# b2 by a broadcast load, zero products ahead of the sums for q, T3's sum on GpSimd, T4 over T2

## The chip, the cores and the metric

One core of a Trainium2 chip. The time is device microseconds of one execution of the whole kernel; lower is better.

## The reference

```python
q_emb = relu(q @ W3 + b3)              # q: 64 x 512, W3: 512 x 1024
v_sum = sum(v, axis=1, keepdims=True)  # v = x: 64 x 128 x 1024
y = (128 * v + v_sum) * q_emb[:, None, :]
out = x + relu(y @ W2 + b2)            # W2: 1024 x 1024, b2: 1024, all float32
```

## The kernel before

**What it computes with.** x is scaled in place, per feature (partition) and batch row: y = scale * x + bias, with scale = 128 * q_emb and bias = v_sum * q_emb. A unit is two batch rows (t = 0, 1), a pair is two units (c = 0, 1): 16 pairs. The two row blocks t and the two halves of the features h make y a 2 x 2 block matrix, and W2 is cut in the same way into b11, b12, b21, b22. Each operand of TensorE is split in two numbers, hi = the value rounded to fp32r (ScalarE) and lo = value - hi (VectorE), and each block product is hi*hi + hi*lo + lo*hi over four slices k: 12 matmuls of 128x128 by 128x512. Pair 0 takes the 16 plain block products (`PLAIN_PRODUCTS`). Pairs 1 to 15 take the 7-product scheme of Strassen and Winograd, 14 products a pair in the order `ORDER` (m = 1, 5, 6, 2, 7, 3, 4, each for c = 0 and 1; "step i" below). It needs four sums of weights: T1 = b12 - b11, T2 = b22 - T1, T3 = b22 - b12, T4 = b21 - T2 up to sign. Each is made once, in fp32, in a staging buffer, and then split into hi and lo. All weights stay in the SBUF for the rest of the run.

**Staging.** Three pairs of halves of 128x1024: `w_halves` (b11, T1, T2), `v_halves` (b12, T3) and `u_halves` (b21, b22, b21 again, T4). `u_halves` are also the buffers `u2_sb` and `m5_sb` of the pairs.

**Order.** Nothing is scheduled by a planner: the order of each engine is written out by hand, with semaphores. The start is: W3 by four slices, the first quarter of x, b11 in four pieces (SyncE's queue); on TensorE four products of zeros (`mark`), the row b2 spread over 128 partitions by a product with a row of ones, then the sums for q (`q_sum(k)`, four of eight before the first product, the others behind it), zero products between and behind them (`WARM_UP`), and then the plain products. ScalarE copies b2 out of PSUM to `b_first` and `b_step`, makes q_emb (`q_relu`), rounds (`cast_w`, `cast_first`), scales (`scale_first`, `scale_usual`) and writes b2 into the banks that a product adds to (`seed_plain`, `seed_p`, `seed_r`). VectorE sums x over its rows (`sums_0`, `scalars_usual`), makes the lo parts (`low_w`, `low_first`, `low`), the sums of weights (`w_sum`) and the results (`plain_result`, `c11` and so on). GpSimd scales three quarters of x and makes b_step - b_first. Every engine works its own list in order; a late instruction holds up all that stands behind it in that list.

Behind `low_first(8)` VectorE's list is: low b22, sum T3, scalars of unit 3 (`scalars_usual(1, 1, 1)`), sum T2, low T3, then pair 1. Ahead of it stand low b12, sum T1, scalars of unit 2, four plain results and low T1. In pair 1, at step 4 both halves of T4 are summed, at step 6 their lo parts follow. Product i = 2 (m = 5, c = 0) needs `seed_r(1, 0)`, which ScalarE does ahead of cast 5 and behind the plain result that VectorE does at step 4; product i = 8 (m = 7, c = 0) needs `save_u2(1, 1, 0)`, which ScalarE does ahead of cast 11.

Of the kernel before, what the change touches and what calls it, by code (L numbers as in the profile page):

```python
# [5 lines left out]
def cond_residual(nc, x_t, x, small_t, b2, w3_t, w2_q, out):  # L6
# [38 lines left out]

    SPLIT = [("b11", 4), ("b21", 2), ("b12", 2), ("t1", 2), ("b22", 2), ("t3", 2), ("t2", 2), ("t4", 2)]
# [8 lines left out]
    with ctx:  # L55
# [3 lines left out]
        def sem(name):  # L59
# [15 lines left out]
        ones = sb("ones", [1, P])  # L75
# [13 lines left out]
        b2_row = w_extra[0:1].rearrange("p k m -> p (k m)")  # L89
# [4 lines left out]
                 "b21": u_halves, "b22": u_halves, "t4": u_halves}  # L94

        small_loaded, b2_loaded = sem("small_loaded"), sem("b2_loaded")
# [13 lines left out]
        table_set, warm_set, ones_set = sem("table_set"), sem("warm_set"), sem("ones_set")  # L110
        marked, b_sent, b_copied, b_seeded, b_step_ready = sem("marked"), sem("b_sent"), sem("b_copied"), sem("b_seeded"), sem("b_step_ready")
# [3 lines left out]
        t1_ready, t2_ready, t3_ready, t4_ready = sem("t1_ready"), sem("t2_ready"), sem("t3_ready"), sem("t4_ready")  # L115
        x0_scaled = [sem(f"x0_scaled{n}") for n in range(QUARTERS)]
# [61 lines left out]
        def _(sp):  # L178
# [7 lines left out]
            def load_half(name, kh, mh, h, loaded):  # L186
                half = slice(h * 2 * MH, (h + 1) * 2 * MH)
                sp.dma_start(STAGE[name][h], w2_q[kh, mh, :, half]).then_inc(loaded[h], 16)
# [10 lines left out]
            load_b11(0)  # L199
            load_b11(1)  # L200
# [7 lines left out]
            for h in range(2):  # L208
                load_half("b21", 1, 0, h, b21_loaded)
# [12 lines left out]
            for h in range(2):  # L222
                sp.wait_ge(w_lo_ready, split("b21", h))
                load_half("b22", 1, 1, h, b22_loaded)

            for h in range(2):
                sp.wait_ge(w_lo_ready, split("b22", h))
                sp.wait_ge(t3_ready, h + 1)
                sp.wait_ge(t2_ready, h + 1)
                load_half("t4", 1, 0, h, b21_again)  # L230
# [46 lines left out]
        def _(pe):  # L277
# [3 lines left out]
            def q_sum(k):  # L281
                pe.wait_ge(w3_loaded[k], 16)
                bank = Q_BANKS[k] if k < KH else 1
                for t in range(QT):
                    last = nc.tensor.matmul(acc[:, bank, k * B:(k + 1) * B], w3_stage[:, k, t], cond_sb[:, t],  # L285
                                            start=k < KH and t == 0, stop=False, skip_group_check=True)
                last.then_inc(q_summed, 1)

            def mark(bank, start=False):

                return nc.tensor.matmul(acc[:, bank], warm[:, :P], warm[:], start=start, stop=False, skip_group_check=True)  # L291

            pe.wait_ge(warm_set, 1)
            for bank in (3, 6, 2, 4):
                mark(bank, start=True)
            pe.wait_ge(ones_set, 1)
            pe.wait_ge(b2_loaded, 16)
            add(acc[:, 3], ones[:], b2_row[:, :MH])
            add(acc[:, 6], ones[:], b2_row[:, MH:]).then_inc(b_sent, 1)
            pe.wait_ge(small_loaded, 16)  # L300
            for k in range(KH):
                q_sum(k)
                if k < KH - 1:
                    mark(4)
            for _ in range(WARM_UP):
                mark(2)
            for n, bank in enumerate(Q_BANKS):
                pe.wait_ge(q_ready, n + 1)
                last = mark(bank)
            last.then_inc(marked, 1)  # L310

            for n, (o, name, bank) in enumerate(PLAIN_PRODUCTS):
                if n > 0:
                    pe.wait_ge(lo_ready, o + 1)
                if n == 0:
                    pe.wait_ge(b_copied, 1)
                if n in (1, 2, 3):
                    pe.wait_ge(b_seeded, n)
                if bank == 6:
                    pe.wait_ge(b_copied, 2)  # L320
                if bank == 7 or bank < 2:
                    pe.wait_ge(b_seeded, {7: 4, 0: 5, 1: 6}[bank])
# [52 lines left out]
        def _(act):  # L375
            def cast_first(n):
                q, c, place = MADE[n]
                act.wait_ge(x0_scaled[n % QUARTERS], 1)
                if n == QUARTERS:
                    act.wait_ge(x0_scaled[0], 2)  # L380
# [4 lines left out]
                if n == 0:  # L385
                    half = KH // 2
                    nc.scalar.copy(a_hi[:, place, :half], quarter(c, q)[:, :half]).then_inc(hi_started, 1)
                    act.wait_ge(x0_scaled[0], 2)
                    nc.scalar.copy(a_hi[:, place, half:], quarter(c, q)[:, half:]).then_inc(hi_ready, 1)
                else:  # L390
                    nc.scalar.copy(a_hi[:, place], quarter(c, q)).then_inc(hi_ready, 1)  # L391
# [63 lines left out]
            def save_m5(p, c):  # L455
                act.wait_ge(prod_done, done_by(p, 5, c))
                if isinstance(p, int) and p == 1:
                    act.wait_ge(w_lo_ready, split("t4", 1))
# [4 lines left out]
            def save_u2(p, parity, c):  # L463
                act.wait_ge(prod_done, done_by(p, 6, c))
                if not (isinstance(p, int) and p == 1):
# [13 lines left out]
            act.dma_start(b2_row, b2).then_inc(b2_loaded, 16)  # L479
# [3 lines left out]
            act.wait_ge(b_sent, 1)  # L483
            nc.scalar.copy(b_first[:], acc[:, 3]).then_inc(b_copied, 1)
            nc.scalar.copy(b_step[:], acc[:, 6]).then_inc(b_copied, 1)
# [7 lines left out]
            act.wait_ge(b_copied, 2)  # L493
# [4 lines left out]
            act.wait_ge(q_ready, KH)  # L498
            seed_plain(4, b_first)
            for k in range(KH, KT):  # L500
                q_relu(k)
            scale_first(2)
            cast_first(2)
# [7 lines left out]
            seed_plain(7, b_step)  # L511
            seed_plain(0, b_step)
# [7 lines left out]
            for h in range(2):  # L520
                cast_w("t1", h, t1_ready, h + 1)
            for n in range(3):
                scale_usual(1, 1, n)
            for c in range(2):
                seed_p(1, 1, c)
            cast_first(8)
            for h in range(2):
                cast_w("b22", h, b22_loaded[h], 16)
            for h in range(2):
# [4 lines left out]
            def pair(p, parity, following=True):  # L534
                first = isinstance(p, int) and p == 1
                for i in range(STEPS):
# [14 lines left out]
                    if first and i == 6:  # L551
# [17 lines left out]
        def _(pool):  # L569
# [7 lines left out]

            for n in (3, 4, 6):
                scale_first(n)

            pool.wait_ge(b_seeded, 6)
# [3 lines left out]
        def _(dve):  # L585
# [115 lines left out]
            nc.vector.memset(ones[:], 1.0).then_inc(ones_set, 1)  # L701
# [3 lines left out]
            for k in range(KH):  # L705
                last = nc.vector.tensor_scalar(x_sb[:, 0, 0, k], x_sb[:, 0, 0, k], scale[:, 0, 0, k:k + 1],
                                               bias[:, 0, 0, k:k + 1], ALU.mult, ALU.add)
                if k % 2 == 1:
                    last.then_inc(x0_scaled[0], 1)
# [5 lines left out]
            low_w("b11", 1)  # L715
            dve.wait_ge(hi_ready, 1)
            low_part(place, KH // 2, KH, quarter(c, q)).then_inc(lo_ready, 1)
            sums_0(1)
            low_w("b11", 2)
            scalars_0(1)  # L720
            low_w("b11", 3)
# [5 lines left out]
            sums_0(4)  # L727
            scalars_0(4)
            low_first(2)
# [13 lines left out]
            for h in range(2):  # L743
                low_w("b12", h)

# [3 lines left out]
            scalars_usual(1, 1, 0, x1_loaded[0], 16)  # L749
            plain_result(4, 0, 0, 0, c11_done)  # L750
            plain_result(5, 0, 1, 0, c21_done)
            for h in range(2):
                low_w("t1", h)
            plain_result(6, 1, 0, 0, c11_done)
            plain_result(7, 1, 1, 0, c21_done)
# [3 lines left out]

            for h in range(2):  # L760
# [11 lines left out]
            def pair(p, parity, loads=None):  # L772
# [3 lines left out]
                for i in range(STEPS):  # L776
# [27 lines left out]
                    if first and i == 6:  # L804
# [58 lines left out]
```

## Time and profile before

| | |
|---|---|
| median of 3 runs | 649.77 us (649.77 to 649.79) |
| profiled execution: time, span | 649.77 us, 648.0 us |
| TensorE busy | 636.9 us, 2795 matmuls |
| VectorE, ScalarE, GpSimd busy | 445.0, 420.9, 7.7 us |
| matmuls of block products | 2712 = 226 products x 12 |

A row of the timeline gives start and length in us, engine, line, operation, what it writes and reads, its shape, how often it stands in a row, and in brackets the idle time ahead of it with what ended it. Matmuls are pipelined: what a matmul costs in a stream is the distance from start to start, not its length.

### The profile page before, as it was taken

Reading aid. Unit: us, or ns where it says so; the run is one execution under the profiler, and the core shown is the slowest. Engines: PE = TensorE matmul, PEld = TensorE weight load, DVE = VectorE, ACT = ScalarE, POOL = GpSimd, SP = SyncE. Lnnn points to the kernel's source line nnn. Section 1 sums busy time; section 2 is a strip of 40 time slices with the busy share of each in tenths; the row PEclk is TensorE's granted clock in tenths of the full one; section 3 lists DMA queues with packets and bytes.
Section 4 is the critical chain, followed back from the end, with each engine's and each line's share of the span. In section 5 each row is a group of like instructions: output and inputs, shape, how many; then the busy total and the mean of one; then the engine's idle time right before and its main releaser. Section 6 shows DMA issues by size and latency. Waiting matters only on the chain.

```text
span 648.0 us, 9257 instructions
## 1 busy us (share of the span) xinstructions
PE 636.9 (98%) x2795; PEld 522.5 (81%) x2796; DVE 445.0 (69%) x675; ACT 420.9 (65%) x902; POOL 7.7 (1%) x17
## 2 busy tenths in 40 slices
PE   9898999999999999999999999999999999999997
PEld 6786778888888888888888888888888888888886
DVE  1788888777576767757677675767767576876633
ACT  2777778765939576593957759395674948668320
POOL 0220000000000000000000000000000000000000
PEclk9999999999999999999999999999999999999999
DMA  8741474637354353735335373433636443360603
GB/s 305 305 177 27 168 244 178 229 147 243 130 194 138 148 168 129 259 129 188 123 150 186 129 256 132 166 123 159 199 129 229 159 150 118 161 218 1 234 25 129
DMA packets 27232, 108.31 MB, mean 167 GB/s; under 512 B 3025, under 2 KB 3153, under 8 KB 23378
## 3 DMA queue, kind: packets, MB, share of 16 engines
q1 hardware_dynamic: 27072, 108.02, 46.5%
q10 hardware_dynamic: 146, 0.14, 0.1%
q8 instruction: 5, 0.08, 0.1%
q14 instruction: 9, 0.07, 0.0%
HBM read 74.59 MB, written 33.55 MB: 167 GB/s over the span
## 4 chain that ended last, share of the span: by engine, by line
PE 88%; ACT 6%; DVE 5%; issue 1%; ACTq 0%; DVEq 0%
PE acc L279 86%; ACT x_sb L409 3%; PE acc L285 2%; DVE vsum L587 1%; DVE w_lo L655 1%; ACT w_hi L428 1%; ACT a_hi L391 1%; DVE a_lo L650 1%; PE acc L291 0%; ACT a_hi L404 0%; DVE w_stage L659 0%; ACT acc L477 0%; DVE xn L663 0%; ACT q_emb L473 0%; DVE m_sb L659 0%
## 5 line engine op out<-in xcount | busy, mean ns | idle before, releaser
L279 PE MATMUL acc<-w_hi,a_hi 128*128 128x512 f32 x904 | 352.6, 390 | 6.4 <-DVE a_lo L639 3.6
L279 PE MATMUL acc<-w_lo,a_hi 128*128 128x512 f32 x904 | 351.7, 389 | 0.0
L279 PE MATMUL acc<-w_hi,a_lo 128*128 128x512 f32 x904 | 351.7, 389 | 0.0
L409 ACT ACTIVATE x_sb<-x_sb,bias,scale 128x128 f32<-128x128 f32 x496 | 204.8, 488 | 12.0 <-DVE bias L595 12.0
L279 PEld LDWEIGHTS acc<-w_hi,a_hi 128*128 128x128 f32 x904 | 169.7, 188 | 44.2 <-DVE a_lo L639 4.4
L279 PEld LDWEIGHTS acc<-w_hi,a_lo 128*128 128x128 f32 x904 | 169.7, 188 | 35.4
L279 PEld LDWEIGHTS acc<-w_lo,a_hi 128*128 128x128 f32 x904 | 169.7, 188 | 34.8
L650 DVE TENSOR_TENSOR a_lo<-x_sb,a_hi 128x512 fp32r<-128x512 f32 x150 | 103.5, 690 | 109.3 <-ACT a_hi L404 108.7
L404 ACT CAST a_hi<-x_sb 128x512 fp32r<-128x512 f32 x150 | 93.5, 623 | 40.1 <-PE acc L279 38.1
L404 ACT CAST a_hi<-s 128x512 fp32r<-128x512 f32 x60 | 37.5, 624 | 73.2 <-PE acc L279 69.1
L587 DVE TENSOR_REDUCE vsum<-x_sb 128x16 f32<-128x2048 f32 (+1 forms) x38 | 73.8, 1942 | 6.8 <-DMA x_sb<-x_t 6.8
L663 DVE SCALAR_TENSOR_TENSOR xn<-acc,xn 128x512 f32<-128x512 f32 x68 | 46.6, 689 | 35.4 <-PE acc L279 35.4
L453 ACT COPY acc<-acc 128x512 f32<-128x512 f32 x30 | 17.1, 571 | 50.1 <-PE acc L279 50.1
L650 DVE TENSOR_TENSOR a_lo<-s,a_hi 128x512 fp32r<-128x512 f32 x60 | 41.3, 688 | 0.1
L679 DVE TENSOR_TENSOR m_sb<-m_sb,acc 128x512 f32<-128x512 f32 x30 | 20.6, 688 | 23.2 <-PE acc L279 21.9
L689 DVE TENSOR_TENSOR u_sb<-u_sb,acc 128x512 f32<-128x512 f32 x30 | 20.6, 688 | 8.4 <-PE acc L279 8.4
L663 DVE SCALAR_TENSOR_TENSOR xn<-m_sb,xn 128x512 f32<-128x512 f32 x30 | 20.6, 686 | 0.2
L629 DVE TENSOR_TENSOR s<-s,x_sb 128x512 f32<-128x512 f32 x30 | 20.6, 686 | 0.1
L663 DVE SCALAR_TENSOR_TENSOR xn<-u_sb,xn 128x512 f32<-128x512 f32 x30 | 20.6, 686 | 0.1
L625 DVE TENSOR_TENSOR s<-x_sb 128x512 f32<-128x512 f32 x30 | 20.6, 686 | 0.0
L631 DVE TENSOR_TENSOR x_sb<-x_sb 128x512 f32<-128x512 f32 x30 | 20.5, 685 | 0.0
L635 DVE TENSOR_TENSOR x_sb<-x_sb,s 128x512 f32<-128x512 f32 x30 | 20.5, 685 | 0.0
(51 smaller groups left out, 195.9 us busy)
## 6 DMA issues: line engine op xcount, KB each, us to landing
xn<-x SPq DMA_DIRECT2D x64, 512.0 KB, 4.0
out<-xn SPq DMA_DIRECT2D x62, 512.0 KB, 4.2
x_sb<-x_t SPq DMA_DIRECT2D x30, 1024.0 KB, 5.0
x_sb<-w_t SPq DMA_DIRECT2D x8, 256.0 KB, 5.4
x_sb<-x_t SPq DMA_DIRECT2D x8, 256.0 KB, 7.8
u_sb<-w_q SPq DMA_DIRECT2D x3, 512.0 KB, 7.5
m_sb<-w_q SPq DMA_DIRECT2D x3, 512.0 KB, 7.6
w_stage<-w_q SPq DMA_DIRECT2D x4, 256.0 KB, 6.2
```

What stands on the lines that cost most here:

```text
L279: return nc.tensor.matmul(dst, lhs, rhs, start=False, stop=False, skip_group_check=True)
L404: nc.scalar.copy(a_hi[:, i % RING], operand(m, 2 * parity + c, c)).then_inc(hi_ready, 1)
L409: last = nc.scalar.activation(x_sb[:, slot, t, k], x_sb[:, slot, t, k], ACT.Identity, bias=bias[:, slot, t, k:k + 1], scale=scale[:, slot, ...
L587: nc.vector.tensor_reduce(vsum[:, slot, t0:t1, k0:k1], x_sb[:, slot, t0:t1, k0:k1], AX.X, ALU.add).then_inc(vsum_ready, 1)
L625: last = nc.vector.tensor_tensor(s, a21, a22, ALU.add)
L629: last = nc.vector.tensor_tensor(s, s, a11, ALU.subtract)
L631: last = nc.vector.tensor_tensor(a21, a11, a21, ALU.subtract)
L635: last = nc.vector.tensor_tensor(a12, a12, s, ALU.subtract)
L650: nc.vector.tensor_tensor(a_lo[:, i % RING], operand(m, 2 * parity + c, c), a_hi[:, i % RING].bitcast(fp32), ALU.subtract).then_inc(lo_rea ...
L663: nc.vector.scalar_tensor_tensor(o, bank, 0.0, o, ALU.max, ALU.add).then_inc(ready, 1)
L679: nc.vector.tensor_tensor(m5_sb[:, c], m5_sb[:, c], p_bank(parity, c), ALU.add).then_inc(c22_summed, 1)
L689: nc.vector.tensor_tensor(u2_sb[:, c], u2_sb[:, c], r_bank(c), ALU.add).then_inc(c12_summed, 1)
```

## The change

- b2 comes in by two broadcast loads on SyncE's queue (`load_b`), 128 partitions x 512 each: `b_first` behind the first piece of b11, `b_step` ahead of b12. The row of ones, its two products and ScalarE's two copies are gone, and so is the wait of SyncE's queue for them. The load of b3 and q (`small_t`) is now the first on ScalarE's queue.
- TensorE starts with eight zero products in a row (one for each bank) in place of four and the two of b2; one more follows each of the four sums for q, and then `WARM_UP` = 11, without waits for q_emb.
- The first quarter of x is scaled by VectorE (two slices) and GpSimd (two slices); its second lo part comes ahead of the lo part of b11's second piece. q_emb's second half is made after quarter 2 is scaled and rounded.
- Product (8, b12) comes after (2, b12). b22 is split ahead of T1; ScalarE rounds quarter 8 and b22 ahead of T1.
- T3's sum runs on GpSimd, ahead of b_step - b_first.
- T4 is made over T2 in `w_halves`, one half at step 5 and one at step 6; it is rounded at step 7 and its lo part is made at step 8. `save_m5` and `save_u2` of pair 1 wait for T4's sum.

```diff
-    WARM_UP = 5
+    WARM_UP = 11
@@ SyncE
             load_first(0)
             load_b11(0)
+            load_b(b_first, 0, b_first_loaded)
             load_b11(1)
...
-            sp.wait_ge(b_sent, 1)
+            load_b(b_step, 1, b_step_loaded)
             for h in range(2):
-                load_half("b12", 0, 1, h, b12_loaded)
+                load_half(v_halves, 0, 1, h, b12_loaded)
@@ TensorE
-            for bank in (3, 6, 2, 4):
-                mark(bank, start=True)
-            pe.wait_ge(ones_set, 1)
-            pe.wait_ge(b2_loaded, 16)
-            add(acc[:, 3], ones[:], b2_row[:, :MH])
-            add(acc[:, 6], ones[:], b2_row[:, MH:]).then_inc(b_sent, 1)
+            for n in range(8):
+                nc.tensor.matmul(acc[:, n], warm[:, :P], warm[:], start=True, stop=True)
             pe.wait_ge(small_loaded, 16)
             for k in range(KH):
                 q_sum(k)
-                if k < KH - 1:
-                    mark(4)
-            for _ in range(WARM_UP):
-                mark(2)
-            for n, bank in enumerate(Q_BANKS):
-                pe.wait_ge(q_ready, n + 1)
-                last = mark(bank)
-            last.then_inc(marked, 1)
+                keep_warm(1)
+            keep_warm(WARM_UP).then_inc(marked, 1)
@@ ScalarE
-            cast_first(0)
+            cast_first_half(0)
+            act.wait_ge(b_first_loaded, 16)
+            seed_plain(3, b_first)
+            cast_first_half(1)
...
+            for n in range(2):
+                scale_usual(1, 1, n)
+            cast_first(8)
+            for h in range(2):
+                cast_w("b22", h, b22_loaded[h], 16)
             for h in range(2):
                 cast_w("t1", h, t1_ready, h + 1)
-            for n in range(3):
-                scale_usual(1, 1, n)
+            scale_usual(1, 1, 2)
@@ GpSimd
+            pool.wait_ge(scalars_first, 1)
+            for k in range(KH // 2, KH):
+                last = nc.gpsimd.tensor_scalar(x_sb[:, 0, 0, k], x_sb[:, 0, 0, k], scale[:, 0, 0, k:k + 1],
+                                               bias[:, 0, 0, k:k + 1], ALU.mult, ALU.add)
+            last.then_inc(x0_scaled[0], 1)
...
+            for h in range(2):
+                pool.wait_ge(b22_loaded[h], 16)
+                pool.wait_ge(w_lo_ready, split("b12", h))
+                pool.wait_ge(t1_ready, h + 1)
+                nc.gpsimd.tensor_tensor(v_halves[h], u_halves[h], v_halves[h], ALU.subtract).then_inc(t3_ready, 1)
@@ VectorE
             for h in range(2):
                 low_w("b12", h)
+            scalars_usual(1, 1, 0, x1_loaded[0], 16)
...
                 w_sum(w_halves, v_halves, w_halves, h, t1_ready)
-            scalars_usual(1, 1, 0, x1_loaded[0], 16)
+            low_first(8)
+            for h in range(2):
+                low_w("b22", h)
             plain_result(4, 0, 0, 0, c11_done)
             plain_result(5, 0, 1, 0, c21_done)
-            for h in range(2):
-                low_w("t1", h)
             plain_result(6, 1, 0, 0, c11_done)
             plain_result(7, 1, 1, 0, c21_done)
-            low_first(8)
-            for h in range(2):
-                low_w("b22", h)
-
-            for h in range(2):
-                dve.wait_ge(w_lo_ready, split("b12", h))
-                dve.wait_ge(t1_ready, h + 1)
-                w_sum(v_halves, u_halves, v_halves, h, t3_ready)
+            for h in range(2):
+                low_w("t1", h)
             scalars_usual(1, 1, 1, x1_loaded[1], 16)
...
-                    if first and i == 4:
-
-                        dve.wait_ge(t2_ready, 2)
-                        for h in range(2):
-                            dve.wait_ge(b21_again[h], 16)
-                            w_sum(u_halves, u_halves, w_halves, h, t4_ready)
-                    if first and i == 6:
+                    if first and i in (5, 6):
+
+                        h = i - 5
+                        dve.wait_ge(w_lo_ready, split("t2", h))
+                        dve.wait_ge(b21_again[h], 16)
+                        w_sum(w_halves, u_halves, w_halves, h, t4_ready)
+                    if first and i == 8:
                         for h in range(2):
                             low_w("t4", h)
```

## Rows read from the trace of the kernel before

**Rows 1.** The page: busy time by engine, and the chain that ended last.
```profile
PE 636.9 (98%) x2795; PEld 522.5 (81%) x2796; DVE 445.0 (69%) x675; ACT 420.9 (65%) x902; POOL 7.7 (1%) x17
PE 88%; ACT 6%; DVE 5%; issue 1%; ACTq 0%; DVEq 0%
```

**Rows 2.** The chain in order of time, its last long piece (start us, us, what).
```profile
95.03 549.73 PE acc L279 x2424
```

**Rows 3.** Waits of TensorE from 0 to 100 us (us in total, times, longest).
```profile
PE acc L279 <- DVE a_lo L639: 3.6, 2, 2.5
PE acc L279 <- DVE a_lo L650: 1.3, 1, 1.3
PE acc L279 <- ACT acc L445: 1.1, 1, 1.1
```

**Rows 4.** Timeline of TensorE, 0 to 25 us.
```profile
1.20 1.89 PE L291 MATMUL acc<-warm 128*128 128x512 bf16 x4 [1.20 <-DVE warm L699]
3.02 3.78 PE L279 MATMUL acc<-w_extra,ones 1*128 1x512 f32 x4
12.96 1.81 PE L285 MATMUL acc<-small_sb,x_sb 128*128 128x64 f32 x8
14.56 2.77 PE L291 MATMUL acc<-warm 128*128 128x512 bf16 x6
17.55 0.66 PE L291 MATMUL acc<-warm 128*128 128x512 bf16 x2 [0.22 <-DVE a_lo L639]
18.28 0.40 PE L279 MATMUL acc<-w_lo,a_hi 128*128 128x512 f32 x1
21.43 3.68 PE L285 MATMUL acc<-small_sb,x_sb 128*128 128x64 f32 x32
```

**Rows 5.** Timeline of ScalarE and VectorE, 14 to 17 us.
```profile
14.81 0.38 ACT L473 ACTIVATE q_emb<-acc,small_sb 128x64 f32<-128x64 f32 x1 [1.65 <-PE acc L285]
15.49 1.12 DVE L706 TENSOR_SCALAR x_sb<-x_sb,scale,bias 128x128 f32<-128x128 f32 x4
16.51 0.69 DVE L655 TENSOR_TENSOR w_lo<-w_stage,w_hi 128x512 fp32r<-128x512 f32 x1
```

**Rows 6.** DMA issues, 5.0 and 7.8 us (KB each, us to landing).
```profile
w_stage<-w_q SPq DMA_DIRECT2D x1, 256.0 KB, 6.8
x_sb<-x_t SPq DMA_DIRECT2D x1, 256.0 KB, 7.4
```

**Rows 7.** Timeline of GpSimd and VectorE, where both work.
```profile
35.72 0.45 POOL L574 TENSOR_SCALAR x_sb<-x_sb,scale,bias 128x128 f32<-128x128 f32 x1
34.78 0.96 POOL L574 TENSOR_SCALAR x_sb<-x_sb,scale,bias 128x128 f32<-128x128 f32 x1
34.80 0.69 DVE L639 TENSOR_TENSOR a_lo<-x_sb,a_hi 128x512 fp32r<-128x512 f32 x1
37.11 1.29 DVE L639 TENSOR_TENSOR a_lo<-x_sb,a_hi 128x512 fp32r<-128x512 f32 x2 [1.62 <-ACT a_hi L391]
38.16 1.39 POOL L582 TENSOR_TENSOR b_step<-b_step,b_first 128x512 f32<-128x512 f32 x1 [1.99 <-ACT acc L477]
39.11 1.53 DVE L655 TENSOR_TENSOR w_lo<-s,w_hi 128x1024 fp32r<-128x1024 f32 x1 [0.70 <-ACT w_hi L428]
40.56 1.21 DVE L655 TENSOR_TENSOR w_lo<-w_extra,w_hi 128x1024 fp32r<-128x1024 f32 x1
```

**Rows 8.** Timeline of VectorE and ScalarE, 52 to 95 us.
```profile
52.80 0.69 DVE L639 TENSOR_TENSOR a_lo<-x_sb,a_hi 128x512 fp32r<-128x512 f32 x1 [1.68 <-ACT a_hi L391]
58.30 2.28 DVE L587 TENSOR_REDUCE vsum<-x_sb 128x16 f32<-128x2048 f32 x1
60.82 4.74 ACT L409 ACTIVATE x_sb<-x_sb,bias,scale 128x128 f32<-128x128 f32 x12 [1.35 <-DVE bias L595]
74.91 0.59 ACT L445 COPY acc<-b_step 128x512 f32<-128x512 f32 x1 [0.58 <-DVE xn L663]
94.35 0.58 ACT L467 COPY u_sb<-acc 128x512 f32<-128x512 f32 x1
```

More of the change, by code:

```diff
@@ L42, in cond_residual @@
                       (4, "b21", 3), (5, "b21", 2), (6, "b21", 4), (7, "b21", 5),
[1 row of a table removed]
[1 row of a table added]
                       (5, "b22", 6), (7, "b22", 7), (4, "b22", 0), (6, "b22", 1)]
-    SPLIT = [("b11", 4), ("b21", 2), ("b12", 2), ("t1", 2), ("b22", 2), ("t3", 2), ("t2", 2), ("t4", 2)]
+    SPLIT = [("b11", 4), ("b21", 2), ("b12", 2), ("b22", 2), ("t1", 2), ("t3", 2), ("t2", 2), ("t4", 2)]
     W_PLACE = {"b11": W_SLOT[1], "b21": W_SLOT[2], "b12": W_SLOT[4], "t1": W_SLOT[5], "b22": W_SLOT[3],
                "t3": W_SLOT[7], "t2": W_SLOT[6], "t4": W_SLOT[4]}
-    WARM_UP = 5
+    WARM_UP = 11
     Q_BANKS = (0, 1, 7, 5)
@@ L93, in cond_residual @@
         STAGE = {"b11": w_halves, "t1": w_halves, "t2": w_halves, "b12": v_halves, "t3": v_halves,
-                 "b21": u_halves, "b22": u_halves, "t4": u_halves}
-        small_loaded, b2_loaded = sem("small_loaded"), sem("b2_loaded")
+                 "b21": u_halves, "b22": u_halves, "t4": w_halves}
+        small_loaded = sem("small_loaded")
+        b_first_loaded, b_step_loaded = sem("b_first_loaded"), sem("b_step_loaded")
         w3_loaded = [sem(f"w3_loaded{s}") for s in range(KT)]
@@ L184, in load_w3, with load_half, load_b @@
                 sp.dma_start(w3_stage[:, k], w3_t[k]).then_inc(w3_loaded[k], 16)
-            def load_half(name, kh, mh, h, loaded):
+            def load_half(halves, kh, mh, h, loaded):
                 half = slice(h * 2 * MH, (h + 1) * 2 * MH)
-                sp.dma_start(STAGE[name][h], w2_q[kh, mh, :, half]).then_inc(loaded[h], 16)
+                sp.dma_start(halves[h], w2_q[kh, mh, :, half]).then_inc(loaded[h], 16)
+            def load_b(dst, h, loaded):
+                sp.dma_start(dst[:], b2[:, h * MH:(h + 1) * MH].broadcast_to([P, MH])).then_inc(loaded, 16)
             def load_xn(u, c, t):
@@ L223, in _ @@
                 sp.wait_ge(w_lo_ready, split("b21", h))
-                load_half("b22", 1, 1, h, b22_loaded)
+                load_half(u_halves, 1, 1, h, b22_loaded)
             for h in range(2):
@@ L284, in q_sum, with keep_warm @@
                 for t in range(QT):
-                    last = nc.tensor.matmul(acc[:, bank, k * B:(k + 1) * B], w3_stage[:, k, t], cond_sb[:, t],
-                                            start=k < KH and t == 0, stop=False, skip_group_check=True)
+                    last = add(acc[:, bank, k * B:(k + 1) * B], w3_stage[:, k, t], cond_sb[:, t])
                 last.then_inc(q_summed, 1)
-            def mark(bank, start=False):
-                return nc.tensor.matmul(acc[:, bank], warm[:, :P], warm[:], start=start, stop=False, skip_group_check=True)
+            def keep_warm(n):
+                for _ in range(n):
+                    last = add(acc[:, 2], warm[:, :P], warm[:])
+                return last
             pe.wait_ge(warm_set, 1)
-            for bank in (3, 6, 2, 4):
-                mark(bank, start=True)
-            pe.wait_ge(ones_set, 1)
-            pe.wait_ge(b2_loaded, 16)
-            add(acc[:, 3], ones[:], b2_row[:, :MH])
-            add(acc[:, 6], ones[:], b2_row[:, MH:]).then_inc(b_sent, 1)
+            for n in range(8):
+                nc.tensor.matmul(acc[:, n], warm[:, :P], warm[:], start=True, stop=True)
             pe.wait_ge(small_loaded, 16)
@@ L314, in _ @@
                     pe.wait_ge(lo_ready, o + 1)
[L315 to L322, printed above, removed]
+                if n < 4:
+                    pe.wait_ge(b_seeded, n + 1)
+                if bank >= 6 or bank < 2:
+                    pe.wait_ge(b_seeded, {6: 5, 7: 6, 0: 7, 1: 8}[bank])
                 place, pieces = MADE[o][2], dict(SPLIT)[name]
@@ L375, in _, with cast_first_half @@
         def _(act):
+            def cast_first_half(h):
+                q, c, place = MADE[0]
+                half = slice(h * KH // 2, (h + 1) * KH // 2)
+                act.wait_ge((x0_started, x0_scaled[0])[h], 1)
+                nc.scalar.copy(a_hi[:, place, half], quarter(c, q)[:, half]).then_inc((hi_started, hi_ready)[h], 1)
             def cast_first(n):
@@ L384, in cast_first @@
                     act.wait_ge(prod_done, (min(old) if n == 7 else max(old)) + 1)
[L385 to L391, printed above, removed]
+                nc.scalar.copy(a_hi[:, place], quarter(c, q)).then_inc(hi_ready, 1)
             def cast(p, parity, i):
@@ L464, in save_u2 @@
                 act.wait_ge(prod_done, done_by(p, 6, c))
-                if not (isinstance(p, int) and p == 1):
+                if isinstance(p, int) and p == 1:
+                    act.wait_ge(t4_ready, 2)
+                else:
                     act.wait_ge(c12_done, 2 * p + c - 1)
@@ L497, in _ @@
             cast_first(1)
-            act.wait_ge(q_ready, KH)
             seed_plain(4, b_first)
+            scale_first(2)
+            cast_first(2)
             for k in range(KH, KT):
                 q_relu(k)
-            scale_first(2)
-            cast_first(2)
+            act.wait_ge(q_ready, KH)
             seed_plain(5, b_first)
@@ L510, in _ @@
             cast_first(5)
-            seed_plain(7, b_step)
-            seed_plain(0, b_step)
+            act.wait_ge(b_step_loaded, 16)
+            for bank in (6, 7, 0):
+                seed_plain(bank, b_step)
             scale_first(7)
@@ L528, in _ @@
                 cast_w("b22", h, b22_loaded[h], 16)
+            for h in range(2):
+                cast_w("t1", h, t1_ready, h + 1)
+            scale_usual(1, 1, 2)
+            for c in range(2):
+                seed_p(1, 1, c)
             for h in range(2):
@@ L550, in pair @@
                             cast_w("t2", h, t2_ready, h + 1)
-                    if first and i == 6:
+                    if first and i == 7:
                         for h in range(2):
@@ L704, in _ @@
             dve.wait_ge(scalars_first, 1)
-            for k in range(KH):
+            for k in range(KH // 2):
                 last = nc.vector.tensor_scalar(x_sb[:, 0, 0, k], x_sb[:, 0, 0, k], scale[:, 0, 0, k:k + 1],
                                                bias[:, 0, 0, k:k + 1], ALU.mult, ALU.add)
-                if k % 2 == 1:
-                    last.then_inc(x0_scaled[0], 1)
+            last.then_inc(x0_started, 1)
             q, c, place = MADE[0]
@@ L714, in _ @@
             low_part(place, 0, KH // 2, quarter(c, q)).then_inc(lo_started, 1)
-            low_w("b11", 1)
             dve.wait_ge(hi_ready, 1)
             low_part(place, KH // 2, KH, quarter(c, q)).then_inc(lo_ready, 1)
+            low_w("b11", 1)
+            low_w("b11", 2)
+            low_w("b11", 3)
             sums_0(1)
-            low_w("b11", 2)
             scalars_0(1)
-            low_w("b11", 3)
             sums_0(2)
@@ L758, in _ @@
                 low_w("b22", h)
+            plain_result(4, 0, 0, 0, c11_done)
+            plain_result(5, 0, 1, 0, c21_done)
+            plain_result(6, 1, 0, 0, c11_done)
+            plain_result(7, 1, 1, 0, c21_done)
             for h in range(2):
-                dve.wait_ge(w_lo_ready, split("b12", h))
-                dve.wait_ge(t1_ready, h + 1)
-                w_sum(v_halves, u_halves, v_halves, h, t3_ready)
+                low_w("t1", h)
             scalars_usual(1, 1, 1, x1_loaded[1], 16)
```

33 lines of the change are left out of this document (8 added, 25 removed), and 2 rows, old and new, of the table PLAIN_PRODUCTS.

## The prediction
> **What bounds the kernel now.** The page comes first: TensorE is busy for 98% of the span and holds 88% of the chain that ended last [rows 1]. The chain in order of time then says where the rest lies: from 95.03 us to the end TensorE works without a gap, 2424 matmuls in 549.73 us, 0.2268 us each [rows 2]. That stretch is the same code in both kernels; it can only move. So the question is how early pair 1's product 8 starts, which before is at 95.03 us. All 2712 matmuls at that pace are 615.1 us; they begin at about 18.0 [rows 4] and end at 644.8, so 11.7 us are lost ahead of 95. The waits of TensorE name 6.0 of them: 3.6 for lo parts of pair 0 (one of 2.5), 1.3 and 1.1 in pair 1 [rows 3]. Some 3.5 are the second four sums for q, which stay [rows 4]. The timelines give the chains behind these waits. The profiled execution took 649.77 us, which is also the median of the runs; 1.77 us lie outside its span of 648.0.
>
> **The sums for q.** Before, four zero products (1.20 to 3.0) and b2's two products (3.02 to 6.8) stand ahead of them. A sum takes 1.6 us there and a zero product 0.43 us, the last sum ends at 14.8 and q_emb is there at 15.2 [rows 4, 5]. The zero product's 0.43 us for 512 columns is the 1.2 GHz level; the real products are 0.23 us apart from 18.28 on and the four later sums take 3.68 / 4 = 0.92 us each, the 2.4 GHz level [rows 4]. So before, all sums ahead of the first product ran at the lower level, and it rose some 3.1 us after TensorE had begun nine zero products in a row at 14.56. After, eight stand in a row at 1.20, 3.4 us of the same work with no thin product behind it. I take the rise at about 4.3, the eight done at 4.5, and then four sums with three zero products between them: 4 x 0.92 + 3 x 0.22 = 4.35, to 8.85. q_emb is ready at 9.25, 5.9 us earlier. The loads allow it: the load issued at 5.0 lands at 11.8 and the one at 7.7 lands at 15.1, five places later, so one of 256 KB takes 0.66 us [rows 6]; W3's fourth slice is six places ahead of the former and lands by 7.8, when its sum is due at 7.9. The Trainium skill (TensorE: Matmul & The Clock Gate, "What's actually happening") has the low clock as the default that activity releases; no row shows whether eight zero products are enough, and that is the first rival.
>
> **Product 0.** VectorE scales two slices (2 x 0.28) and makes b11's first lo part, to 10.75, and x's first, to 11.1. Twelve zero products at 0.215 end at 11.45, where product 0 starts. GpSimd's two slices cost 0.45 each when alone, but it sat out VectorE's subtraction at 34.8 (0.96 in place of 0.45) although it had begun first [rows 7]. So I let it begin at 11.1 when VectorE pauses: 12.0, second rounding to 12.45, then b11's second piece: rounded 12.95, lo part 13.66. Lower bound 0.9 us earlier, if GpSimd is not held. Pieces 3 and 4 land 0.66 later than before for the broadcast, at 12.4, and follow at 14.25 and 14.9. Product 0 ends at 15.7, the four sums for q at 19.4 (before 25.1). Both b loads are 256 KB: 0.66 us each in the queue, under others' slack; that both halves of b2 are no longer copied takes 1.1 us from ScalarE, which idled there.
>
> **Pair 0.** Products follow at 12 x 0.2268 = 2.72 us: product 2 at 22.15 where before it was at 29.0. I followed each list with durations of its rows. The smallest margins: lo part 4 is ready some 0.2 us ahead of product 4, lo part 8 three us ahead of product 11. The 2.5 us wait is gone, since quarter 8 is rounded before T1 and used one product later; the other wait (1.1) goes because VectorE has the lo part by 21.3. Product 8 ends at 41.2, product 15 at 60.2.
>
> **T3 on GpSimd.** It frees VectorE of 2 x 1.14 us. Its own price no row shows. Nearest is the 512-wide subtraction: it began at 38.16, VectorE was busy to 38.40, it ended at 39.55: 1.15 us alone; twice that is 2.3 for 1024, upper bound 2 x 1.39 = 2.8. I take 2.25. And it holds VectorE: the lo part at 39.11 took 1.53 where its twin took 1.21 [rows 7]. Rounding 8 must wait for product 8: 41.2 to 41.85. T3's first half runs 39.7 to 41.95 in VectorE's pause, lo part 8 ends at 42.65, and as b22's rounding is not out until 42.85, GpSimd gets in with the second half, to 44.9: 2.0 us lost on VectorE. Bounds: nothing, if VectorE comes first, and 2.8. Behind it b_step - b_first (1.15) is queued, and it alone is behind it; I take that it finds VectorE's plain results (one input from PSUM) and costs nothing.
>
> The Trainium skill (SBUF — State Buffer, "Who interferes with whom") says that a VectorE instruction with two SBUF inputs and a GpSimd instruction that reads SBUF exclude each other whole, and that the order of issue decides who waits. By that rule b_step - b_first, issued at 44.9 while lo b22's first half starts, goes ahead of the second half. The 34.8 us pair speaks against it. This is a rival below.
>
> **VectorE and ScalarE to pair 1.** From 44.9 on VectorE works through: lo b22 2.3, four plain results 2.4, lo T1 2.3, scalars of unit 3 2.4 [the sum alone is 2.28, rows 8], to 54.2. ScalarE then has twelve scalings, 4.7 [rows 8], rounding 0 (59.5), four scalings, rounding 1 (61.6), T2's roundings 1.9, four scalings 1.6, rounding 2 (65.65). VectorE: lo 2 (66.3), sum (67.1), lo 3 (67.7), plain result 12 (68.3); seed_r (69.0). Products 0 and 1 of the pair start on time, product 2 is due at 60.2 + 5.44 = 65.7 and waits until 69.0: a new stall of 3.3 us. Before, that seed ended at 75.5 [rows 8], so product 2 is 6.6 us earlier. T4 no longer stands behind it, so seed_r(1) is in time and the wait of 1.1 is gone. From 68.3 on, VectorE has 7.6 us of steps 4 to 7 with T4 and then 2.4 of scalars; ScalarE behind them three times four scalings, three roundings and three saves, 7.5: save_u2 is done at 85.8 (before 94.93). Product 8 is due at 69.0 + 6 x 2.72 = 85.3 and starts at 85.85.
>
> **The sum.** 95.03 - 85.85 = 9.2 us. 649.77 - 9.2 = 640.6 us, ratio 0.986. The early clock moves the whole of pair 0 by some 6 us; in pair 1 VectorE's list, not TensorE's, then sets the time, so what GpSimd blocks is paid one for one.
>
> **Rivals.**
> - *The clock stays at 1.2 GHz through the sums* (0.16). For it: before, four zero products in a row did not raise it, and neither did 8 us of sums with single ones between. Against it: nine did. Then the eight end at 4.6, the four sums at 12.3, twelve zero products at 16.4 to 17.4, product 0 at 20.1, the sums at 23.8: 4.4 us behind the forecast, 645.0 at most, 644.0 at least.
> - *GpSimd does not hold VectorE* (0.10). T3's second half falls beside the plain results. VectorE gains 2.0: 638.6; with the early start of product 0 also 637.7, with all bounds 637.
> - *GpSimd's b_step also goes first* (0.10): 1.15 more, 641.8.
> - *The broadcast load is slow* (slower; 0.02). Its 128 partitions read one row of 2 KB. It stands ahead of b11's second piece, which lands at about 10.0 and is wanted at 12.45. Each us over 2.4 is paid in full; at 0.66 + 2.4 + 9.2 = 12.3 us for the load it is no gain, and beyond it slower. Against it: rows of 256 KB at 0.66, and the 2 KB a partition is the size of the others.
> - *Nothing moves* (0.03): lists that meet in pair 1 so late that the early start is given back. For it: VectorE bounds pair 1. Against it: its list is 2.3 us shorter and begins 6 us earlier.
>
> **How the numbers follow.** The forecast has 0.59, the rivals 0.16, 0.10, 0.10, 0.02, 0.03. Likeliest 640.6. The range goes from 636.9 (no blocking, all bounds) to 645.2 (the clock stays low), and leaves out some 0.07. 0.2% is 1.3 us, about what a measurement can tell from no change. Faster by more: 0.59 + 0.16 + 0.10 + 0.10 = 0.95; same 0.03; slower 0.02.
>
> **What would show it.** Sums for q 0.92 us each from 4.5 on and q_emb at 9.3: the clock; 1.6 each: the first rival. Product 0's second slice at 13.7 if GpSimd is held, 12.8 if not. No waits of TensorE from 20 to 60. GpSimd's T3: two of 2.25 us, and a lo part of b22 that is 3.2 in place of 1.2. A wait of 3.3 us ahead of pair 1's product 2, behind ScalarE's seed. The last long piece of the chain from 85.85. The prediction is wrong if the clock is not up, if T3 takes over 2.8 us a half, or if a stall comes up in pair 0 that I have let pass with margins of 0.2.

## The result and the profile after

The changed kernel takes 644.35 us (median of 8 runs, 643.42 to 647.92) where the kernel before takes 649.77: ratio 0.9923, 95% interval 0.9911 to 0.9934. It is faster, inside the forecast range of 636.9 to 645.2, but by 5.4 us where 9.2 were forecast. A second thing changed: the kernel before repeats within 0.08 us, the changed one spreads over 4.5. (One run of the kernel before, 1190.6 us at a granted clock of 0.81, stands apart and is compared with nothing.) The profiled execution took 644.10 us, with a span of 642.3.

The page of the changed kernel, answering to [rows 1]:

```profile
PE 632.9 (99%) x2799; PEld 520.8 (81%) x2799; DVE 446.0 (69%) x670; ACT 420.5 (65%) x902; POOL 18.9 (3%) x21
PE 86%; DVE 6%; ACT 5%; issue 1%; POOL 1%; DVEq 0%; ACTq 0%
```

Its chain in order of time, the last long piece (start us, us, what), answering to [rows 2]:

```profile
92.06 547.00 PE acc L283 x2412
```

2412 matmuls are 201 products, so this piece begins with pair 1's product 9. Before, product 9 began at 95.03 + 2.72 = 97.75. The difference, 5.7 us, is the whole difference of the two profiled executions (649.77 - 644.10); nothing is won or lost behind it. Where TensorE waits ahead of it (0 to 100 us, answering to [rows 3]):

```profile
PE acc L283 <- DVE a_lo L655: 2.3, 1, 2.3
PE acc L283 <- issue: 1.4, 1, 1.4
PE acc L300 <- DVE warm L704: 1.2, 1, 1.2
PE acc L283 <- DVE w_lo L660: 0.9, 1, 0.9
PE acc L283 <- ACT u_sb L460: 0.2, 1, 0.2
```

The waits of pair 0 are gone but for 0.9 in product 0. In pair 1 there are now 2.3 us ahead of product 0 and 1.4 ahead of product 2. (This view counts from the end of the matmul before. Counted from where the next matmul was due to start, as the text does from here on, they are 2.5 and 1.5 us, and a "3.0" is 3.2.) The second is put down to issue, time for which the profile shows no releaser; but ScalarE's seed, below, ends at 72.10 and product 2 starts at 72.20.

TensorE's timeline at the start, answering to [rows 4], and behind the first wait of pair 1:

```profile
1.19 3.59 PE L300 MATMUL acc<-warm 128*128 128x512 bf16 x8 [1.19 <-DVE warm L704]
4.58 1.80 PE L283 MATMUL acc<-small_sb,x_sb 128*128 128x64 f32 x8
6.49 1.00 PE L283 MATMUL acc<-small_sb,x_sb 128*128 128x64 f32 x8
13.83 0.50 PE L283 MATMUL acc<-w_hi,a_hi 128*128 128x512 f32 x1 [0.87 <-DVE w_lo L660]
16.02 3.68 PE L283 MATMUL acc<-small_sb,x_sb 128*128 128x64 f32 x32
...
64.58 0.63 PE L283 MATMUL acc<-w_lo,a_hi 128*128 128x512 f32 x1
65.00 0.63 PE L283 MATMUL acc<-w_hi,a_lo 128*128 128x512 f32 x1
65.43 0.63 PE L283 MATMUL acc<-w_hi,a_hi 128*128 128x512 f32 x1
```

The first sum for q still takes 1.6 us, the second 0.84 and a zero product behind it: the clock is up from about 6.2 us. From 64.6 to 67.6 matmuls of block products are 0.43 us apart again, the 1.2 GHz level. The windows view (busy us of TensorE, weight loads, VectorE, ScalarE and GpSimd, granted clock, DMA) has the same:

```profile
45.00:60.00 15.00, 15.00 (x68) 12.44 (x67) 15.00 (x14) 9.37 (x18) 4.24 (x2) 1.00 0.02 7
60.00:75.00 15.00, 11.30 (x41) 8.52 (x41) 13.04 (x18) 12.84 (x27) 0.00 (x0) 0.89 0.58 203
```

GpSimd's timeline, 22 to 50 us (answers to [rows 7]):

```profile
22.13 4.25 POOL L567 TENSOR_SCALAR x_sb<-x_sb,scale,bias 128x128 f32<-128x128 f32 x4 [0.23 <-DVE bias L600]
40.97 3.22 POOL L584 TENSOR_TENSOR s<-u_sb,s 128x1024 f32<-128x1024 f32 x1 [11.65 <-DVE w_stage L664]
44.15 2.86 POOL L584 TENSOR_TENSOR w_extra<-m_sb,w_extra 128x1024 f32<-128x1024 f32 x1
46.97 2.27 POOL L587 TENSOR_TENSOR b_step<-b_step,b_first 128x512 f32<-128x512 f32 x1
```

VectorE in the same stretch:

```profile
43.42 1.31 DVE L644 TENSOR_TENSOR a_lo<-x_sb,a_hi 128x512 fp32r<-128x512 f32 x1 [1.50 <-ACT a_hi L381]
44.66 3.43 DVE L660 TENSOR_TENSOR w_lo<-u_sb,w_hi 128x1024 fp32r<-128x1024 f32 x1
48.01 2.31 DVE L660 TENSOR_TENSOR w_lo<-m_sb,w_hi 128x1024 fp32r<-128x1024 f32 x1
```

Read the two side by side: they take turns (the expectations below call this meeting at the port). T3's first half, held until T1's second sum is done at 41.92, ends at 44.19, then lo 8 (issued 43.42) ends at 44.73, T3's second half at 47.01, lo b22's first half at 48.09, b_step at 49.24, lo b22's second half at 50.32. Each ends one own length (2.3, 0.6, 2.3, 1.1, 1.15, 1.1) behind the one ahead of it. Lo 8 and the two lo parts of b22 take VectorE 7.05 us where they cost 0.69 + 1.22 + 1.21 = 3.12: 3.9 us lost. T3's two halves cost it 2.8 of them (0.6 and 2.2), where the sum itself would take VectorE 2.3; b_step, queued behind T3, costs the other 1.1.

ScalarE in pair 1 (answers to [rows 8]): the seed that product 2 waits for and the save that product 9 waits for.

```profile
71.51 0.59 ACT L435 COPY acc<-b_step 128x512 f32<-128x512 f32 x1 [0.58 <-DVE xn L668]
91.36 0.56 ACT L460 COPY u_sb<-acc 128x512 f32<-128x512 f32 x1
```

### The profile page after: what moved, and what is told of

Its sections match the earlier page's. It is cut to its first block, busy times and chain, and to the rows that moved or that the text cites. A ratio compares the mean times of both kernels' runs of the same rounds, so it can differ in the third digit from the quotient of the medians.

```text
span 642.3 us, 9265 instructions
## 1 busy us (share of the span) xinstructions
PE 632.9 (99%) x2799; PEld 520.8 (81%) x2799; DVE 446.0 (69%) x670; ACT 420.5 (65%) x902; POOL 18.9 (3%) x21
## 4 chain that ended last, share of the span: by engine, by line
PE 86%; DVE 6%; ACT 5%; issue 1%; POOL 1%; DVEq 0%; ACTq 0%
PE acc L283 86%; ACT x_sb L399 3%; DVE w_lo L660 2%; DVE vsum L592 1%; DVE a_lo L655 1%; DVE xn L668 1%; POOL x_sb L567 1%; ACT a_hi L381 1%; PE acc L300 1%; ACT w_hi L418 1%; ACT acc L470 0%; DVE w_stage L664 0%; ACT a_hi L394 0%; POOL x_sb L574 0%; ACT q_emb L466 0%
```

## The experiments

Twelve variants ran. Times are medians of 4 to 10 runs beside runs of the kernel before (medians 649.75 to 649.79) on the same chip. No run takes the reordering in pair 0 by itself (b22 ahead of T1, product (8, b12) one place later).

**Four zero products at the start.** The other banks are cleared by the zero products between the sums; twelve still follow.

```diff
-            for n in range(8):
-                nc.tensor.matmul(acc[:, n], ..., start=True, stop=True)
+            for bank in Q_BANKS:
+                zero(bank)
...
                 q_sum(k)
-                keep_warm(1)
+                zero((2, 3, 4, 6)[k])
```

> Changed kernel with four zero products ahead of the first sums for q in place of eight; the other four banks are cleared by the zero products between the sums; twelve stand behind the sums as before. Theory (the eight in a row raise the clock): the sums take 1.6 us each, q_emb is ready near 12.5 us in place of 10.0, product 0 starts at 16 to 17.5 us in place of 12.0, the whole comes out at 648 us. Rival (the clock rises early anyway, b2's thin products having kept it down in the kernel before): no change from 644.3.

647.54 us (ratio 0.9961, 0.9947 to 0.9975). The sums take 1.6 us each, product 0 starts at 15.95 in place of 12.04. TensorE's timeline, this variant:

```profile
1.20 1.89 PE L300 MATMUL acc<-warm 128*128 128x512 bf16 x4 [1.20 <-DVE warm L707]
4.67 1.97 PE L283 MATMUL acc<-small_sb,x_sb 128*128 128x64 f32 x8 [1.59 <-DMA small_sb<-small_t]
6.86 1.81 PE L283 MATMUL acc<-small_sb,x_sb 128*128 128x64 f32 x8
```

So the four further zero products are worth 3.2 of the 5.4 us, as the medians have it; product 2 of pair 1 starts 3.1 us later (75.31 for 72.20). Taking b2's thin products away without them does not raise the clock.

**The kernel before with eight zero products.**

```diff
             for bank in (3, 6, 2, 4):
                 mark(bank, start=True)
+            for _ in range(4):
+                mark(2)
```

> Kernel before with eight zero products at the start in place of four, nothing else. Theory (the clock and with it all of the start move, and every list behind moves along): b2's two products take half of 3.7 us, the sums 0.92 us each, q_emb ready at 11.3 in place of 15.2, end 3.9 us earlier: 645.9 us. Rival (the lists of VectorE and ScalarE, or loads, set the time in pair 1, so the early start is given back): 648 or more.

Neither: six of ten runs at 648.3, four at 651.5 (ratio 0.9994, 0.9979 to 1.0009). The profiled execution is one of the four; TensorE's timeline:

```profile
4.72 3.78 PE L279 MATMUL acc<-w_extra,ones 1*128 1x512 f32 x4
8.43 1.97 PE L285 MATMUL acc<-small_sb,x_sb 128*128 128x64 f32 x8
```

There the clock did not come up: b2's products take 3.7 us and the sums 1.6 each, all 1.7 us later, and the end is 1.7 us later too. The six runs have no profile; that the clock came up in them is a guess. Their mean granted clock, 0.992 in each, is not that of the four (0.997 to 1.000), so it did take another course in them, but where is not shown. The expectation of 645.9 fell in either case. The rival's 648 or more fits the six: that an early start was partly given back in pair 1 is not excluded. What is shown is that the zeros alone, with b2's products still behind them, gain 1.5 us in some runs and lose 1.7 in others.

**b_step ahead of T3 on GpSimd** (the two tasks change places in its list).

> Changed kernel with b_step - b_first ahead of T3's sums on GpSimd. Theory (each GpSimd instruction that reads the SBUF holds up VectorE's two-input instructions; b_step's costs the second lo part of b22 1.1 us, and VectorE's list sets pair 1): that lo part takes 1.2 us in place of 2.3, seed_r 1.1 us earlier, 643.2 us. Rival (VectorE's list is not what sets the time): 644.3.

644.32 us (ratio 0.9908, 0.9878 to 0.9938; runs 641.60 to 644.94). The mechanism is as expected, in VectorE's timeline of this variant:

```profile
44.88 3.43 DVE L660 TENSOR_TENSOR w_lo<-u_sb,w_hi 128x1024 fp32r<-128x1024 f32 x1
48.24 1.21 DVE L660 TENSOR_TENSOR w_lo<-m_sb,w_hi 128x1024 fp32r<-128x1024 f32 x1
```

Product 2 starts at 71.34 in place of 72.20. The median did not follow. In the profile the single wait ahead of product 2 is now 3.2 us and the clock falls behind it, where nothing hides it: from 71.34 on 2496 matmuls take 567.40 us, against 566.1 at 0.2268.

**T3's sum on VectorE.**

```diff
             for h in range(2):
                 low_w("b22", h)
+            for h in range(2):
+                dve.wait_ge(w_lo_ready, split("b12", h))
+                dve.wait_ge(t1_ready, h + 1)
+                w_sum(v_halves, u_halves, v_halves, h, t3_ready)
```

> Changed kernel with T3's sum back on VectorE, behind the lo parts of b22. Theory (GpSimd costs VectorE 3.9 us between 43 and 50 us and saves it 2.3): VectorE's list is 1.6 us shorter, seed_r at 70.5 in place of 72.1, 642.7 us. Rival (moving the sum off VectorE is a gain): 2.3 us longer, 646.6.

643.19 us (ratio 0.9900, 0.9882 to 0.9918). The lo parts take their own length again, and product 2 is 1.24 us earlier. (b_step now meets b12's lo part at 34 us, as in the kernel before, for 0.3 us.) VectorE's timeline and then TensorE's, this variant:

```profile
44.45 1.23 DVE L654 TENSOR_TENSOR w_lo<-u_sb,w_hi 128x1024 fp32r<-128x1024 f32 x1 [0.26 <-ACT w_hi L418]
45.59 1.22 DVE L654 TENSOR_TENSOR w_lo<-m_sb,w_hi 128x1024 fp32r<-128x1024 f32 x1
```

```profile
70.96 0.77 PE L283 MATMUL acc<-w_hi,a_hi 128*128 128x512 f32 x1 [3.01 <-issue]
71.52 0.63 PE L283 MATMUL acc<-w_lo,a_hi 128*128 128x512 f32 x1
71.95 0.63 PE L283 MATMUL acc<-w_hi,a_lo 128*128 128x512 f32 x1
```

Again the clock falls behind the wait: 0.43 us from 71.5 to 73.6.

**Zero products in the waits.** First on the changed kernel, nine ahead of pair 1's product 0 and five ahead of product 1; then on the variant with T3 on VectorE, six and thirteen.

```diff
+                if first and i < 2:
+                    for _ in range((9, 5)[i]):
+                        add(dst, warm[:, :P], warm[:])
+                    pe.wait_ge(lo_ready, made(p, i))
```

> Changed kernel with nine zero products ahead of pair 1's product 0 and five ahead of product 1, in the time in which TensorE waits. Theory (the waits of 2.5 and 1.5 us lower the clock for a stretch of varying length, which makes the spread of the changed kernel's runs of 643.4 to 647.9): no matmul of block products at 0.43 us, spread under 0.3 us, median 643.8 to 644.2, since ScalarE's seed for product 2 at 72 us is later than the products even at the low clock. Rival (the spread comes from GpSimd and VectorE meeting at the port): the spread stays.

644.46 us, 643.66 to 645.42: no change. The wait ahead of product 2 was still 2.05 us long and the clock fell behind it, at 73.3. Five were too few; this run did not test the theory.

> T3's sum on VectorE (as t3_vector), and six zero products ahead of pair 1's product 0, thirteen ahead of product 1, in TensorE's waits of 1.5 and 3.2 us. Theory (a wait of TensorE lowers the clock behind it, and behind the last wait that is paid in full): no product at 0.43 us a matmul, product 8 at 87.5, product 9 at 90.75 by ScalarE's save_u2, 642.7 us, spread under 0.3 us. Rival (the clock falls there whatever TensorE does, or zeros don't count): 643.2 and a spread of 1 us as t3_vector.

642.55 us (ratio 0.9891, 0.9874 to 0.9907), 641.53 to 642.87, with a mean granted clock of 1.000 in all four runs. No stretch of products runs at 0.43 us. The windows view of TensorE, this variant:

```profile
60.00:75.00 15.00, 15.00 (x68) 1.00 0.50 190
```

and T3 on VectorE without the zeros:

```profile
60.00:75.00 15.00, 10.67 (x40) 0.89 0.47 185
```

The wait that is left is ScalarE's save ahead of product 9 (0.2 us). But the spread is 1.3 us, not under 0.3. Two parts of it are visible in the profiles. The first sum for q takes 0.95 us here and 1.6 in the changed kernel's profile, so the moment at which the clock comes up differs by 0.7 us from one execution to the next. And GpSimd's scaling of quarter 4, the same code in both, takes 2.27 us here and 4.25 there. GpSimd's and VectorE's timelines, this variant:

```profile
21.59 2.27 POOL L572 TENSOR_SCALAR x_sb<-x_sb,scale,bias 128x128 f32<-128x128 f32 x4 [0.23 <-DVE bias L599]
22.13 0.69 DVE L591 TENSOR_REDUCE vsum<-x_sb 128x4 f32<-128x512 f32 x1 [0.64 <-DMA x_sb<-x_t]
38.66 1.22 DVE L663 TENSOR_TENSOR w_stage<-w_extra,w_stage 128x1024 f32<-128x1024 f32 x1
```

The last line is T1's second sum: it ends at 39.88, where it ends at 41.92 in the changed kernel. The changed kernel and seven variants have a profile with quarter 4 on GpSimd: it took 4.24 to 4.29 us in six, 2.27 here and 1.74 in the variant with x's first quarter on VectorE. So rounding 0 of pair 1 starts 1.3 us earlier here than in the profile without the zeros (59.49 for 60.82), ahead of any zero product in pair 1: what the zeros are worth can be read from the medians alone.

**Quarter 4 scaled by VectorE.**

```diff
-            for n in (3, 4, 6):
+            for n in (3, 6):
...
             scalars_0(4)
+            dve.wait_ge(scalars_first, 5)
+            for k in range(KH, KT):
+                last = nc.vector.tensor_scalar(...)
+            last.then_inc(x0_scaled[4], 1)
```

> Changed kernel with quarter 4 of pair 0's x scaled by VectorE, right behind its scalars, in place of GpSimd, where it took 4.25 us for four slices that cost 1.8 alone. Theory (GpSimd, held off by VectorE, delayed ScalarE's rounding 4 and through ScalarE's list rounding 8 by 0.95 us): rounding 4 near 25, rounding 8 at 41.9 in place of 42.8, seed_r 0.9 us earlier, 643.4 us. Rival (the delay is slack): 644.3 or, with VectorE's 1.1 us more, 645.

643.97 us (ratio 0.9921, 0.9894 to 0.9949; 642.58 to 646.59): against the changed kernel's 0.9923 unclear. In its profile rounding 8 starts at 41.97 in place of 42.79, now held by product 8 itself. But T1's second sum ends 1.9 us earlier, at 40.02, and product 2 starts at 70.46 in place of 72.20; some 0.3 us of both is the clock's earlier rise. Then the clock falls behind a wait of 3.2 us and takes 1.6 us back (2496 matmuls in 567.65 us). ScalarE's and VectorE's timelines, this variant:

```profile
41.97 0.62 ACT L381 CAST a_hi<-x_sb 128x512 fp32r<-128x512 f32 x1 [0.99 <-PE acc L283]
38.80 1.22 DVE L664 TENSOR_TENSOR w_stage<-w_extra,w_stage 128x1024 f32<-128x1024 f32 x1
```

**All of x's first quarter on VectorE.** It scales four slices, GpSimd none.

> Changed kernel with all four slices of x's first quarter scaled by VectorE. Theory (GpSimd's two slices, held off by VectorE's two, take 1.7 us to 12.1): scaled at 11.4, product 0's second slice at 13.2 in place of 13.8, all of pair 0 0.6 us earlier, 643.7. Rival (GpSimd relieves VectorE there): product 0 later, 644.6.

643.80 us (ratio 0.9917, 0.9897 to 0.9937). Product 0's second slice starts at 13.28 in place of 13.83, as expected, though 0.2 us of it is the clock's earlier rise; the median is too near to tell. In this profile, too, GpSimd was quick at quarter 4 (1.74 us), and the wait ahead of product 2 is 3.2 us with the lower clock behind it.

**T4 back at step 4.**

```diff
-                    if first and i in (5, 6):
-
-                        h = i - 5
...
+                    if first and i == 4:
+                        for h in range(2):
...
```

> Changed kernel with both halves of T4 summed at step 4, as in the kernel before, still in w_halves. Theory (T4 at step 4 stands ahead of plain result 13 and so of seed_r(1)): that seed 2.3 us later, at 75.6, product 3 waits 0.7 us, the list up to save_u2 is as long as before; 644.4 to 645. Rival (T4's place carries the gain of the change): 2.3 us slower, 646.6.

644.53 us (ratio 0.9917, 0.9904 to 0.9930), no difference from the changed kernel. Product 3 does wait, 1.3 us, and the waits at products 8 and 9 are gone for it: T4's place moves a wait.

**Combinations.** T3 and quarter 4 on VectorE with one and twelve zero products; the same with all of the first quarter; and the same (without the latter) with pair 1's lists reordered.

> T3's sum and the scaling of quarter 4 both on VectorE, with one zero product ahead of pair 1's product 0 and twelve ahead of product 1. Theory (GpSimd's work at the shared port is paid by VectorE's and ScalarE's lists, and the two losses add): seed_r at 69.1 us in place of 72.1, product 9 at 89.0, 641.0 us, no matmul of products in pair 1 at 0.43 us. Rival (the second is slack once the first is gone): 642.5 as t3v_zeros.

642.10 us (ratio 0.9883, 0.9869 to 0.9898). Product 9 starts at 89.81, not 89.0, and 0.3 us later than in the profile with T3 alone on VectorE and the zeros (89.48). But that is the profile in which GpSimd was quick at quarter 4 by itself, so the two do not show whether the second gain is slack; the medians, 642.10 and 642.55, are too near to tell.

> As t3q4_zeros, and all four slices of x's first quarter scaled by VectorE: three of GpSimd's tasks back on VectorE (it keeps quarters 3 and 6 and b_step), one and twelve zero products in pair 1. Theory (each task of GpSimd that reads the SBUF beside VectorE's list costs more than it saves): product 0's second slice 0.6 us earlier and pair 0 with it, 641.6 us. Rival (ScalarE's list in pair 1 sets the time by now): 642.1 as t3q4_zeros.

641.95 us (ratio 0.9880, 0.9864 to 0.9897), 641.47 to 642.35: the fastest, not told from the one before it.

> As t3q4_zeros, with one and four zero products, and pair 1's lists reordered: plain results 12 to 15 at steps 2 to 5 in place of 4 to 7, seed_r at steps 3 and 4, the sums over unit 4 and 5's rows at steps 9 and 11 in place of 7 and 9, T4's lo parts at step 9, ScalarE's scalings of pair 2 at steps 11 to 13, two each. Theory (in pair 1 the time is set by the order of the lists, above all by what stands ahead of seed_r and save_u2): product 2 at 67.1 us, no wait at products 8 and 9, 638.2 us. Rival (the sum of VectorE's and ScalarE's work sets it, so the waits come back in pair 2): 640 to 641.

642.62 us (ratio 0.9900, 0.9882 to 0.9918). Product 2 was no longer the wait; others were, seen in the waits of TensorE from 50 us on:

```profile
PE acc L283 <- ACT acc L448: 0.9, 1, 0.9
PE acc L283 <- ACT u_sb L465: 0.9, 1, 0.9
PE acc L283 <- issue: 0.6, 1, 0.6
```

The last of them is at 99 us, later than any in the other variants. Neither number came (638.2, and 640 to 641 for the rival), but the waits came back as the rival has it: what is put ahead of one task is put behind another, and the work of both engines in pair 1 has to be done.

## Why the prediction was right, and what it mis-sized

**The clock: right, and the largest term.** The eight zero products brought the clock up ahead of the sums, as the variant with four shows (3.2 us, by the medians). It came at about 6.2 us in place of 4.3, so q_emb was ready at 10.0 and not 9.25. The first sum stayed at 1.6 us.

**Product 0: right.** GpSimd was held off by VectorE, 1.7 us for two slices; the second slice started at 13.83 (13.7), the later sums ended at 19.5 (19.4).

**Pair 0: right for TensorE, mis-sized for the list behind it.** Product 15 ended at 61.0 (60.2). But the forecast has no price for GpSimd's scaling of quarter 4 beside VectorE; it took 4.25 us, with three lo parts of VectorE in that time, where four slices cost 1.8 alone. It held rounding 4 (26.41), and with ScalarE's list b12's rounding, T1's sums and rounding 8, which ended at 43.4 for 41.85. What counts is T1's second sum, since T3's first half on GpSimd is held until it is done: it ended at 41.92, where I had that half begin at 39.7. In the profiles in which GpSimd was quick at quarter 4 or did not have it, the sum ended at 39.67 to 40.20, and at 41.10 in the variant with the lists reordered, whose later sums for q ended 0.9 us behind those of its nearest kin (19.8 for 18.9).

**T3 on GpSimd: price right, order wrong.** One half costs 2.28 us alone (44.73 to 47.01), I had taken 2.25. The step that failed is that b_step "finds VectorE's plain results (one input from PSUM) and costs nothing". What I held against the other order was one pair of rows [rows 7, the pair at 34.8]. In fact the two engines took turns in the order of issue, as the Trainium skill says (SBUF — State Buffer, "Who interferes with whom"); lo 8 lost 0.6, lo b22 2.2 and 1.1, together 3.9 us where I had 2.0. That was the rival at 641.8, which I gave 0.10. The two variants without T3 or without b_step there remove 3.9 and 1.1 us of it.

**The two together.** T3's second half ended at 47.01 for 44.9, 2.1 us late, which T1's late sum covers (41.92 for 39.7); b_step added 1.1, and the second lo part of b22 ended at 50.3 for 47.2. To 0.1 us those are the 3.1 us by which seed_r came late (72.1 for 69.0). Product 8 came 3.0 us late (88.85 for 85.85). Product 9, forecast one product behind, at 88.6, came at 92.06, 3.5 us late, by a second save of ScalarE that cost another 0.5.

**The clock behind a wait: missing.** I had put a new wait of TensorE, 3.3 us, in pair 1 and counted its length alone. In all five profiles with a wait of 3.2 us ahead of product 2 the clock falls behind it and 1.3 to 1.6 us more are paid (567.40 to 567.65 us for 2496 matmuls, for 566.1). In the profile of the changed kernel it fell at 64.6 us and the wait for the seed hid it, so it does not explain that profile's 5.7 us. Filling the waits took the median from 643.19 to 642.55 and the granted clock to 1.000; the two intervals overlap, so the size is less sure than the mechanism.

**T4's place:** as forecast it keeps seed_r(1) in time, and as not forecast it is worth nothing in the sum.

**The spread** was not forecast. The moment of the rise (0.7 us: in eleven profiles with eight zero products the first sum took 0.93 to 1.60 us) and GpSimd's quarter 4 (T1's second sum 2 us earlier or later) are shown parts. They are not all: with quarter 4 on VectorE the times still spread over 4.0 us (642.58 to 646.59). The changed kernel's one run at 647.9 is near the variant with four zero products (647.5), which would fit a rise that did not come; it was not profiled, so that stays open.

## What to carry to other kernels

Price work that is moved to GpSimd by whom it meets: where both engines read two operands from the SBUF, every instruction here was paid by the other at full length in the order of issue. T3's sum saved VectorE 2.3 us and cost it 2.8, and 1.1 more for the task queued behind it. Work put there can also make the time uneven, as quarter 4 did. Zero products ahead of thin ones can buy the higher clock early (eight did here and four did not), and waits that a change creates on TensorE can lose it again just behind them: behind 3.2 us it cost 1.3 to 1.6 us more, so fill such waits or add that. When two engines' lists set a stage, unloading a list helped here; reordering it moved the wait.

## What the runs showed of the hardware that was not expected

- TensorE's clock: in the kernel before, waits of 2.6, 1.3 and 1.5 us left the products at 0.23 us; in the changed kernel matmuls 0.43 us apart follow its wait of 2.5 us, but begin 1.1 us behind it (straight behind the same wait in the variant with T4 at step 4). In the variant with nine and five zeros they follow a wait of 2.05 us. Whether a wait costs the clock is not told by its length alone.
- Turns at the port: GpSimd and VectorE alternated five times in a row between 41.9 and 50.3 us, each beginning when the other's instruction was done, though VectorE's were ready back to back.
- GpSimd's same four slices of quarter 4 took 4.24 to 4.29 us in six profiles, 2.27 and 1.74 us in two. In both of the two VectorE had waited for a load until 22.1 or 22.3 us, but so it had in one of the six (22.10); what tips it is not shown.
- Two groups of times, 648.3 and 651.5 us, in one program (the kernel before with eight zero products), on one chip in one session, with nothing between them.
